# A graph aggregation on one Trainium2 core: sums of a destination group alternate between two PSUM banks

## What is computed

```python
h = (x @ W).reshape(n, heads, out_c)
ex = jnp.exp(e - m[dst])
z = jax.ops.segment_sum(ex, dst, num_segments=n)
alpha = ex / (z[dst] + 1e-16)
msg = h[src] * alpha[:, :, None]
out = jax.ops.segment_sum(msg, dst, num_segments=n)
```

## Time and profile before

| what | value |
|---|---|
| median of 3 runs | 3213.5 us |
| the profiled execution's own time | 3225.58 us |
| its span, from first to last instruction | 3223.8 us |
| aggregation of layer 0 | 651.7 to 1318.0 us of the span |
| aggregation of layer 1 | 1893.9 to 2553.0 us of the span |
| mean granted TensorE clock | 0.724 of full speed |

### The profile page before, as it was taken

How to read it: one execution, slowest core, us unless ns; L and a number is a source line. 1 busy time by engine, 2 the same in 40 slices (tenths; PEclk the granted TensorE clock), 3 DMA queues, 4 the chain that set the end, 5 groups by cost and what they waited for, 6 DMA issues and landing times. The chain is left out here.

```text
span 3223.8 us, 50021 instructions
## 1 busy us (share of the span) xinstructions
PE 1833.6 (57%) x14982; PEld 1228.4 (38%) x14983; DVE 1385.2 (43%) x2368; ACT 772.8 (24%) x2073; POOL 1391.2 (43%) x1323
## 2 busy tenths in 40 slices
PE   4578874056555655363679315555554474199980
PEld 3444552033333333232345203333333274177760
DVE  7656556555556556593763330000000185011115
ACT  3201100023333333351012003333332321033330
POOL 0355563266667767343000035555555433412216
PEclk9788886556666667676899655656666655599995
DMA  4311110168778778423327768888888683145449
GB/s 142 85 32 47 32 27 17 61 221 255 249 248 258 250 248 253 154 60 87 102 66 245 239 224 269 274 268 270 270 270 271 218 315 126 32 160 166 157 147 395
DMA packets 182781, 580.89 MB, mean 180 GB/s; under 512 B 49268, under 2 KB 51315, under 8 KB 182473
## 3 DMA queue, kind: packets, MB, share of 16 engines
q0 software_dynamic: 81744, 351.62, 34.7%
q1 hardware_dynamic: 75790, 159.71, 15.0%
q10 hardware_dynamic: 25200, 69.03, 5.6%
HBM read 473.74 MB, written 106.49 MB: 180 GB/s over the span
## 5 line engine op out<-in xcount | busy, mean ns | idle before, releaser
L1314 PE MATMUL acc<-ring,work 128*32 128x192 f32 x3904 | 350.7, 493 | 310.1 <-ACT work L1376 197.1
L1230 POOL DMA_INDIRECT ring<-feat_tab,islot x392 | 419.4, 1070 | 236.5 <-issue 108.8
L1269 DVE TENSOR_TENSOR work<-iota_f,dst_rel 128x224 f32<-128x224 f32 x112 | 44.1, 394 | 701.8 <-PE acc L1314 328.4
L639 POOL DMA_INDIRECT work<-score_tab,islot x224 | 230.7, 1030 | 168.8 <-DVE islot L692 102.0
L1314 PEld LDWEIGHTS acc<-ring,work 128*32 128x32 f32 x3904 | 147.8, 143 | 377.8 <-issue 341.2
L1314 PE MATMUL acc<-work 128*32 128x192 f32 (+1 forms) x2208 | 198.3, 461 | 162.4 <-ACT work L1376 111.1
L1380 ACT ACTIVATE work<-work 32x192 f32<-32x192 f32 x800 | 287.6, 360 | 10.7
L1230 POOL DMA_INDIRECT work<-feat_tab,islot x224 | 234.5, 1047 | 127.4 <-issue 54.3
L596 PE MATMUL acc<-wg,work 128*128 128x384 f32 x600 | 225.8, 527 | 30.2 <-issue 28.1
L1314 PE MATMUL acc<-big,work 128*32 128x192 f32 x1744 | 168.7, 475 | 120.1 <-ACT work L1376 87.2
L1230 POOL DMA_INDIRECT big<-feat_tab,islot x168 | 179.4, 1068 | 97.5 <-issue 41.0
(11 more groups left out here) (351 smaller groups left out, 3270.8 us busy)
## 6 DMA issues: line engine op xcount, KB each, us to landing
slot_out<-ring SPq DMA_DIRECT2D x57, 384.0 KB, 2.3
agg_raw<-work ACTq DMA_DIRECT2D x50, 388.0 KB
ring<-agg_raw SPq DMA_DIRECT2D x50, 388.0 KB
feat_tab<-work ACTq DMA_DIRECT2D x50, 384.0 KB
ring<-lo_rows SPq DMA_DIRECT2D x49, 256.0 KB
edges<-in_w_fast SPq DMA_DIRECT2D x28, 384.0 KB
edges<-in_w_slow SPq DMA_DIRECT2D x28, 384.0 KB
edges<-in_w_hebb SPq DMA_DIRECT2D x28, 384.0 KB
```

The source lines that it names most:

```text
L639: pool.indirect_dma_start(sg[:, h, k * H:(k + 1) * H], None, score_tab[0], bass.IndirectOffsetOnAxis(ap=islot[:, h * 8 + k:h * 8 + k + 1], ...
L1230: pool.indirect_dma_start(rows[k][:, 0:C], None, feat_tab[l], bass.IndirectOffsetOnAxis(ap=islot[:, h * UN + k:h * UN + k + 1], axis=0)).t ...
L1269: ins = V.tensor_tensor(out, near.to_broadcast([P, BATCH, WIN]), dst_rel[:, cols].unsqueeze(2).to_broadcast([P, BATCH, WIN]), ALU.is_equal)
L1314: m = nc.tensor.matmul(sums_ps[c * WIN:(c + 1) * WIN, 0:n], hot, row[:, c * CHUNK:c * CHUNK + n], start=start, stop=True, skip_group_check ...
```

## The change

Two banks of `acc` are used in turn (`BANKS = 2`): group b is summed in bank b mod 2. `flushed` starts one higher, so that the opening of a group waits for the copies of the group before the last. There are two `onehot_x`, and ACT makes each one group earlier. The copy to `stage` is gone: ACT's five copies read the bank directly, and the last of them raises `flushed`. The closing matmul writes to another PSUM tensor (`tps`). Because a matmul's destination is fixed in an instruction, PE keeps the bank in a register, and each tile's matmuls stand in the program twice, under an If on that register; the same for the opening matmuls.

```diff
-        onehot_x = agg_part(WIN)
-        stage = [agg_part(CHUNK + ZC) for _ in range(2)]
-        zeros = stage[1]
+        onehot_x = [agg_part(WIN) for _ in range(2)]
+        zeros = agg_part(CHUNK + ZC)
...
+                    def place(bank, c, a, z):
+                        return acc[c * WIN:(c + 1) * WIN, bank, a:z]
+
+                    def added(i, k, t, j):
+                        if k % BATCH == 0:
+                            pe.wait_ge(hot_ready, i * 2 + (k // BATCH + 1))
+                        if l == 0:
+                            pe.wait_ge(msg_ready, t + 1)
+                        else:
+                            pe.wait_ge(row_in[k], i * 16 + 16)
+                        sums(onehot[:, k, :], k, t, False, j).then_inc(tile_mm, 1)
+
+                    def opened(b, k, t, j):
+                        pe.wait_ge(open_ready, b)
+                        pe.wait_ge(flushed, b)
+                        sums(onehot_x[j], k, t, True, j).then_inc(open_mm, 1)
...
-                        nc.tensor.matmul(acc[0:WIN, 1, 0:1], iota_f[:, 0:WIN], iota_f[:, 0:1], start=True, stop=True,
+                        nc.tensor.matmul(tps[0:WIN, 0, 0:1], iota_f[:, 0:WIN], iota_f[:, 0:1], start=True, stop=True,
...
-                            sums(onehot[:, k, :], k, t, False).then_inc(tile_mm, 1)
+                            bank = pe.snap(bank_reg, min_val=0, max_val=BANKS - 1)
+                            with pe.If(bank > 0):
+                                added(i, k, t, 1)
+                            with pe.Else():
+                                added(i, k, t, 0)
...
-                                    pe.wait_ge(open_ready, b)
-                                    pe.wait_ge(flushed, b)
-                                    sums(onehot_x, k, t, True).then_inc(open_mm, 1)
+                                    pe.reg_mov(bank_reg, b & (BANKS - 1))
+                                    bank = pe.snap(bank_reg, min_val=0, max_val=BANKS - 1)
+                                    with pe.If(bank > 0):
+                                        opened(b, k, t, 1)
+                                    with pe.Else():
+                                        opened(b, k, t, 0)
...
+                    act.sem_inc(flushed, BANKS - 1)
+
+                    def next_hot(b, j):
...
-                        act.wait_ge(open_mm, b)
-                        nc.scalar.activation(onehot_x, hot_open[:, ds(b * WIN, WIN)], ACT.Copy).then_inc(open_ready, 1)
+                        act.wait_ge(open_mm, b - 1)
+                        nc.scalar.activation(onehot_x[j], hot_open[:, ds(b * WIN, WIN)], ACT.Copy).then_inc(open_ready, 1)
...
-                            nc.scalar.activation(stage[w % 2], sums_ps, ACT.Copy).then_inc(flushed, 1)
-                            next_hot(q + 2)
-                            act.wait_ge(flushed, q + 1)
                             for c in range(4):
                                 nc.scalar.activation(raw[sl][w * WIN:(w + 1) * WIN, c * CHUNK:(c + 1) * CHUNK],
-                                                     stage[w % 2][c * WIN:(c + 1) * WIN, 0:CHUNK], ACT.Copy)
-                            m = nc.scalar.activation(raw[sl][w * WIN:(w + 1) * WIN, C:ROW],
-                                                     stage[w % 2][zp:zp + WIN, CHUNK:CHUNK + ZC], ACT.Copy)
-                            m.then_inc(blk_ready, 1)
-                        act.wait_ge(blk_ready, b * WPB + WPB)
+                                                     acc[c * WIN:(c + 1) * WIN, w % BANKS, 0:CHUNK], ACT.Copy)
+                            nc.scalar.activation(raw[sl][w * WIN:(w + 1) * WIN, C:ROW],
+                                                 acc[zp:zp + WIN, w % BANKS, CHUNK:CHUNK + ZC], ACT.Copy).then_inc(flushed, 1)
+                            next_hot(q + 3, (w + 3) % 2)
+                        act.wait_ge(flushed, b * WPB + (WPB + BANKS - 1))
```

More of the change, by code:

```diff
@@ L18 @@
 WPB = P // WIN
+BANKS = 2
 TURNS = NT // UN
@@ L1210, in aggregate @@
                 sem(n + L) for n in ("msg", "hot", "open_hot", "tile_mm", "open_mm", "ones", "open_table"))
-            closed, flushed, blk_ready, zero_set, batch_mm = (
-                sem(n + L) for n in ("closed", "flushed", "blk_ready", "zero_set", "batch_mm"))
+            closed, flushed, zero_set, batch_mm = (sem(n + L) for n in ("closed", "flushed", "zero_set", "batch_mm"))
             st_out = [sem(f"st_out{j}" + L) for j in range(2)]
@@ L1216, in aggregate @@
             w_in, chain_v, idx_ready, tick_p = sem("w_in" + L), sem("dve" + L), sem("idx" + L), sem("tick_p" + L)
-            sums_ps = acc[:, 0, 0:CHUNK + ZC]
             zp = 0 if l == 0 else 3 * WIN
@@ L1308, in _, with sums @@
                 def _(pe):
-                    def sums(hot, k, t, start):
+                    def place(bank, c, a, z):
[12 more added lines that the diff above has]
+                        sums(onehot_x[j], k, t, True, j).then_inc(open_mm, 1)
+                    def sums(hot, k, t, start, bank):
                         row = rows[k]
@@ L1313, in sums @@
                             n = CHUNK + ZC if l == 1 and c == 3 else CHUNK
-                            m = nc.tensor.matmul(sums_ps[c * WIN:(c + 1) * WIN, 0:n], hot, row[:, c * CHUNK:c * CHUNK + n],
+                            m = nc.tensor.matmul(place(bank, c, 0, n), hot, row[:, c * CHUNK:c * CHUNK + n],
                                                  start=start, stop=True, skip_group_check=True)
@@ L1318, in sums @@
                         if l == 0:
-                            m = nc.tensor.matmul(sums_ps[0:WIN, CHUNK:CHUNK + ZC], hot, ex[:, ds(t, 1), :].rearrange("p a h -> p (a h)"),
+                            m = nc.tensor.matmul(place(bank, 0, CHUNK, CHUNK + ZC), hot, ex[:, ds(t, 1), :].rearrange("p a h -> p (a h)"),
                                                  start=False, stop=True, skip_group_check=True)
@@ L1327, in _ @@
                     for c in range(4):
-                        m = nc.tensor.matmul(sums_ps[c * WIN:(c + 1) * WIN, :], zeros[:, 0:WIN], zeros, start=True, stop=True,
+                        m = nc.tensor.matmul(acc[c * WIN:(c + 1) * WIN, 0, 0:CHUNK + ZC], zeros[:, 0:WIN], zeros, start=True, stop=True,
                                              skip_group_check=True)
@@ L1331, in _ @@
                     bits_reg = [pe.alloc_register(f"bits{l}")]
+                    bank_reg = pe.alloc_register(f"bank{l}")
+                    pe.reg_mov(bank_reg, 0)
                     regs = [pe.alloc_register(f"open{l}_{j}") for j in range(2)]
@@ L1375, in body @@
                             act.wait_ge(closed, q + 1)
[L1376 to L1378 removed]
                             for c in range(4):
                                 nc.scalar.activation(raw[sl][w * WIN:(w + 1) * WIN, c * CHUNK:(c + 1) * CHUNK],
[L1381 to L1385 removed]
+                                                     acc[c * WIN:(c + 1) * WIN, w % BANKS, 0:CHUNK], ACT.Copy)
[3 more added lines that the diff above has]
+                        act.wait_ge(flushed, b * WPB + (WPB + BANKS - 1))
                         act.dma_start(agg_raw[l][ds(b * P, P), :], raw[sl]).then_inc(st_out[sl], 16)
                     act.wait_ge(table_ready, 1)
[L1388 to L1389 removed]
+                    next_hot(1, 1)
+                    next_hot(2, 0)
                     blocks(act, body)
```

9 lines of the change are left out of this document (removed).

## The result

The changed kernel took 3223.5 us (median of 20 runs, 3214.4 to 3233.5), the kernel before 3210.7 us in runs taken beside it: a ratio of 1.0036, 95% interval 1.0018 to 1.0053. That is 12.8 us slower where I had forecast 35 us faster. Its profiled execution has a span of 3225.0 us and a granted clock of 0.673, before 0.724. Two later runs of the unchanged pair gave 1.0056 (1.0028 to 1.0085) and 1.0036 (1.0012 to 1.0059).

What follows compares the result with a forecast made beforehand. The prediction took PE, late in a chain of waits, to bound both layers. Its terms -30 (layer 1), -4 (layer 0) and -1 gave -35 us, 3178.5 us for the median, range 3116 to 3227, at 35%.

Steps and rivals of the forecast that it cites:

- What bounds the kernel: Both aggregations: a chain of waits with PE late; POOL alone would need 495 us in layer 1, 573 in layer 0.
- Hand-over removed: Group borders: PE no longer waits for the copy just begun; 20 to 48 us gained per layer, -30 us for layer 1.
- Branches added on PE: Each tile: compare-and-branch plus jump, 0.27 us; layer 0's group to 5.9 us, -4 us there with the hand-over gain.
- My count over the single periods: Layer 0's 99 periods, each less 0.48 us but held at 5.9 or more: adds 33 us, the slow bound.
- Layer 1's cover: Layer 1 tiles: 1.28 us each covers the sequencer's 0.9 us, so no branch cost was entered there.
- The sum: Whole kernel: -30 for layer 1, -4 for layer 0, -1 for the last groups' copies; -35 us in all.
- the signs that I named: PE's waits for ACT nearly vanish; layer 1 copies 6.1 to 6.3 us apart; POOL's idle there falls some 30 us.
- The third: Rival, 18%: PE's sequencer bounds layer 0, tiles 0.9 us apart, few periods under 5.9 us; 3226 to 3252 us.
- The second: Rival, 23%: nothing moves; the hand-over's 0.48 us is spent inside the tiles, time within 10 us of 3213.
- The first: Rival, 17%: PE's granted clock rises, POOL becomes the bound; 2988 us at the full, about 3100 for half.
- The fourth: Rival, 7%: the longer loop leaves the instruction buffer and is read again each turn; +129 us, 3308 to 3343.

Runs made afterwards that it cites:

- the longer hand-over: Kernel before, one bank, no branches, ACT copying directly from the bank before handing it back: 1.011 on the first kind of chip, 1.003 and 1.001 on the second.
- the half variants: Kernel before with half the matmuls of each tile (1.000, 0.998) or half the bytes of each gather (0.994), on the second kind of chip.
- branches alone: Kernel before, one bank and old copy, with only the change's branches choosing between identical arms: 1.030 on the first kind of chip, 1.072 twice on the second.
- without later gathers: Gathers in only the first of 28 turns, in either kernel: kernel before 2636 us, changed kernel 3081 us; the unedited kernel before took 2869 us.
- its three variants: Changed kernel with half the matmuls of each tile (1.063), half the bytes of each gather (1.067), or gathers in only the first of 28 turns (1.071).

## Why the prediction failed, step by step

**What bounds the kernel.** PE is late in both layers, as the prediction said, but only on the first kind of chip, the one it was made for; on the second POOL's 498 us are the layer. Nothing in a single trace could tell me that. (This is read from the longer hand-over and the half variants; the kernel before itself left no trace on the second kind.)

**Hand-over removed: right.** The bounds were 20 and 48 us for each layer, and 30 was taken for layer 1. The second bank gave 43 and 31 us against branches alone. PE's waits for ACT went to nothing as foretold. The reason was only half right: I named the copy of 0.34 us and its latency, while what the second bank hides is mostly the late signal of the closing matmul: 1.1 us more of copying at each border cost 0.26 and 0.18 us for a group (6.80 and 6.63 us against 6.54 and 6.45, in layer 0 and layer 1).

**Branches added on PE: the step that failed, by its size.** I took 0.27 us for each tile, 0.9 us per tile in all, 5.9 us for a group of layer 0. Measured is +0.42 us in layer 0 and +0.54 us in layer 1 for each tile (medians; means 0.40 and 0.49), so a tile of layer 0 takes the sequencer 1.07 us and a group 6.64 us. The border was priced nearly right: 0.9 + 0.75 + 1.55 = 3.2 us, measured 3.3; three tiles at some 0.2 us each are what the group has above 5.9. And 6.64 us is above the 6.54 us that a group took before the change, so in layer 0 the branches eat all that the second bank saves and more, 61 us against 43, where the forecast had -4 for both together. My count over the single periods was too coarse as well: with 6.64 in place of 5.9 it would give +79 us, and layer 0 grew by 17.

I had counted the compare-and-branch and a jump. The sequencer's rows of the changed kernel have two more instructions at each tile, a register move (the copy of the bank register) and, in layer 1, a register operation that works out the wait value again in each arm of the branch, which straight code had worked out once:

```profile
L1355 PEldq MOVE  x728: 3/29/698, 648.7 to 2550.1; - x182
...
L1315 PEldq FUSED_REGOPS  x392: 3/37/699, 1906.4 to 2550.3; - x196
...
L1356 PEldq COMPARE_BRANCH  x1176: 3/169/1239, 641.1 to 2550.5; - x196
```

The move takes 29 ns, but the next instruction begins some 90 ns after its start, and it is this distance that a sequencer at its limit pays. The last row mixes three things, and its median of 169 ns is not the price of the branch: its 1176 records are 784 branches and 392 jumps at the end of the first arm. The single records of layer 1 without later gathers (where the line is L1362) sort them. In the arm in which the branch falls through it takes 65 to 78 ns, and the next instruction begins 0.12 us after its start; then the jump behind that arm's matmuls takes some 169 ns and pays 0.23. In the other arm the branch is taken, lasts 200 to 217 ns and pays 0.26, and no jump is recorded, though the listing has one behind it too. With 0.09 for the move and 0.09 for the wait value a tile pays 0.53 us in one arm and 0.44 in the other, which is the 0.49 us by which the mean grew. Layer 0 worked out a wait value at each tile before the change too, and so pays 0.1 us less. I had the listing of the change before me, and should have counted its rows and not its meaning. The Trainium skill, "Advanced Engine Details and Errata", section "Control Flow Timing", gives about 108 ns for a compare-and-branch and 51 ns for a jump; an estimate from that page's two figures is 0.16 us a tile, and the trace disagrees, with 0.26 us in one arm and 0.35 in the other.

**Layer 1's cover: the second step that failed.** For layer 1 I wrote nothing, since "a tile takes 1.28 us, which covers 0.9". That was a misreading. I had divided the 5.1 us from the opening to the next bank copy by four tiles, but the closing matmul of that group starts long before the copy at 2120.64 us, as the trace of the kernel before already shows:

```profile
2118.09 0.27 PE L1324 MATMUL acc<-iota_f 128*32 128x1 f32 x2
```

So 2.3 us of the 5.1 lie behind its modelled end, and the tiles without a border are issued 0.56 us apart in that layer (median). The 1.28 us were no property of the array: the same matmuls pass at 0.39 us each tile without gathers on the second kind. It was the late signals of the first kind. Under them the branches hide in great part: from the kernel before to branches alone the 294 tiles of layer 1 without a border take 110 us more (0.63 to 1.00 us each, means), while the 98 distances across a border take 84 us less (4.7 to 3.9 us). What is left is +25 us where I had written nothing.

**The sum.** Forecast -30 for layer 1, -4 for layer 0 and -1; measured -9 and +17 by the copies (6.48 to 6.39 us and 6.56 to 6.73), and on the chip with all three kernels second bank -81, branches +94, in all +13. Of the signs that I named, PE's waits for ACT went; but the copies of layer 1 begin 6.39 us apart and not 6.1 to 6.3, and POOL's idle time there fell by 10.8 us and not by 30.

**The rivals.** The third, the sequencer as bound of layer 0, is what happened, in layer 0 as it said ("tiles 0.9 us apart": 1.1; periods under 5.9 us: 31 of 99, where it was 50) and partly in layer 1 too. I gave it 18% and priced it at +13 to +39 us. The time came out at its lower end by two errors against each other: layer 0 lost 17 us and not 33 to 58, and layer 1 gained 9 and not 20. The second, nothing moves, gives nearly the right time for the wrong reason: two effects of 81 and 94 us nearly cancel. The Trainium skill, "TensorE: Matmul & The Clock Gate", section "HAM oscillation", stood beside it, with its kernel in which double buffering in PSUM gave no further gain once its matmuls were continuous. This kernel is not in that state, with 252 us of waits at the borders of layer 1, and here the second bank gave 81 us. The first was wrong: the granted clock fell where it had to rise. The fourth was wrong: 24 packets on the instruction queue in the whole run, for 28 turns of each loop. By the room of 2048 instructions that the Trainium skill, "Runtime: NRT & Kernel Launch", section "Instruction fetch mechanics", gives TensorE the loop of some 1613 fits, and the trace agrees.

**What stays open.** Why PE's signals come late on the first kind of chip. It is not the bytes of the gathers. Whether half of the matmuls, or no gathers, would bring them in time was asked, but those runs fell on the second kind. They are not slower engines all round: ACT's copy takes 0.337 us and a gather of layer 1 0.96 us on either kind. The changed kernel itself did not run on the second kind; that it would lose 6 to 7% there is an estimate from its three variants (1.063, 1.067, 1.071) and from branches alone (1.072, twice).

## What to carry to other kernels

A run-time branch around each tile costs every instruction that it adds to the sequencer, from start to start, the copies of registers and the values worked out again in each arm among them: count the rows of the listing, and compare the sequencer's time for a whole group with the group's time, not a branch with a tile. If a wait at a border is much longer than the work it waits for (here 2.8 us on average for a copy of 0.34 us), look at when that work could start before you price its removal: here the start itself came late, a second bank hid part of that, and the length of the work hardly mattered. And a bound read from one trace is the bound on that chip: before trusting one, see whether the engine that comes next has room.

## What the runs showed of the hardware

The same program took 3211 to 3221 us in three sets of runs and 2869 to 2877 us on three other chips, 11% less. On the slower kind the closing signal of a group in layer 1 came 2.5 us (median) after the modelled end of its matmul, on the other 0.1 us. With a branch at each tile the granted clock of layer 0 was 0.50 from end to end on both kinds (1.2 GHz), with half the matmuls too, and it didn't bound the time: half the matmuls at that clock took the same. Without gathers both kernels ran on one chip, first the kernel before, whose tiles follow each other at 0.65 us in layer 0 and 0.39 in layer 1, then the changed one, at 1.07 and 0.93 us:

```profile
560.00:1014.40 454.40, 296.46 (x5110) 208.72 (x5110) 363.52 (x475) 216.38 (x693) 7.84 (x9) 0.88 0.08 30
1590.00:1960.00 370.00, 241.02 (x4128) 116.73 (x4128) 46.10 (x139) 205.25 (x694) 1.90 (x2) 0.93 0.18 60
```

```profile
577.00:1242.00 665.00, 455.87 (x5110) 289.50 (x5110) 363.18 (x474) 167.54 (x597) 0.00 (x0) 0.50 0.04 15
1818.00:2410.00 592.00, 424.66 (x4128) 135.30 (x4128) 46.09 (x139) 157.03 (x596) 0.00 (x0) 0.55 0.10 35
```

The granted clock was 0.88 and 0.93 before the change and 0.50 and 0.55 after it. So in these runs the lower clock comes with the sequencer's slower issue; it is a sign of that pace and not its cause.
